# Turning nine of twelve quantized x tiles on VectorE inside the attention units instead of on TensorE after them

## The reference, cut to what matters

```python
xn = _layernorm(x, axis=-1)
s  = attention(xn)            # 32 query heads of 16, one shared key and value head, causal, then @ wo
h  = _linear8bit(xn, W1, b1)  # rows of xn quantized to 8 bits (absmax/127), columns above a threshold kept whole
y  = _linear8bit(h, W2, b2)
return x + s * silu(y)
```

## Time and profile before

| | us |
|---|---|
| median of 3 runs (lowest, highest) | 790.0 (789.12, 792.09) |
| the profiled execution, its own time | 790.14 |
| its span in the profile | 788.4 |
| busy: PE, DVE | 753.5 (96%), 650.9 (83%) |
| busy: ACT, POOL | 395.5 (50%), 273.5 (35%) |

### The profile page before, as it was taken

How to read it: one execution, slowest core, us unless ns; L and a number is a source line. 1 busy time by engine, 2 the same in 40 slices (tenths; PEclk the granted TensorE clock), 3 DMA queues, 4 the chain that set the end, 5 groups by cost and what they waited for, 6 DMA issues and landing times. The chain is left out here.

```text
span 788.4 us, 11979 instructions
## 1 busy us (share of the span) xinstructions
PE 753.5 (96%) x4133; PEld 568.3 (72%) x4133; DVE 650.9 (83%) x1115; ACT 395.5 (50%) x670; POOL 273.5 (35%) x349
## 2 busy tenths in 40 slices
PE   5999999999999999999899999999998999999995
PEld 4877665556767666766578878778886888888884
DVE  7988999999899999996448568597858998599957
ACT  4454066777776776677834435454563333132212
POOL 7213135555555555555432212222100000027404
PEclk9999699999999999999999999999998999999998
DMA  7431302332332233234465677646323778427972
GB/s 258 156 111 54 78 21 78 88 81 78 93 106 84 83 84 83 82 83 124 134 228 172 153 239 209 187 101 166 82 53 121 236 245 269 148 89 237 337 279 107
DMA packets 93772, 110.71 MB, mean 140 GB/s; under 512 B 43136, under 2 KB 50320, under 8 KB 92176
## 3 DMA queue, kind: packets, MB, share of 16 engines
q1 hardware_dynamic: 93712, 109.95, 45.8%
HBM read 56.43 MB, written 40.37 MB: 123 GB/s over the span
## 5 line engine op out<-in xcount | busy, mean ns | idle before, releaser
L933 DVE TENSOR_REDUCE rowmax<-ps 128x2 f32<-128x512 f32 (+3 forms) x384 | 210.3, 591 | 19.5 <-PE ps L1010 17.9
L854 ACT ACTIVATE probs<-ps 128x512 f32<-128x512 f32 (+1 forms) x352 | 174.9, 558 | 71.1 <-PE ps L1023 69.7
L1010 PE MATMUL ps<-km,stack 128*128 128x256 f32 (+3 forms) x512 | 149.7, 347 | 2.3 <-PEq L195 1.9
L1023 PE MATMUL ps<-stack,ks 128*128 128x512 f32 (+1 forms) x352 | 131.4, 383 | 2.8 <-ACT probs L854 2.7
L1010 PEld LDWEIGHTS ps<-km,stack 128*128 128x128 f32 (+1 forms) x512 | 94.2, 198 | 43.0 <-DVE rowmax L933 23.6
L836 POOL TENSOR_SCALAR_AFFINE_SELECT probs<-probs 128x512 f32<-128x512 f32 x128 | 81.0, 641 | 77.9 <-ACT probs L854 76.4
L1872 PE MATMUL ps<-big_h 128*128 128x512 f32 x256 | 99.9, 390 | 1.6 <-issue 1.2
L1874 PE MATMUL ps<-big_h,big_l 128*128 128x512 f32 x256 | 99.6, 389 | 0.0
L1873 PE MATMUL ps<-big_l,big_h 128*128 128x512 f32 x256 | 99.6, 389 | 0.0
L1036 PE MATMUL ps<-probs,vones 128*32 128x512 f32 (+3 forms) x1024 | 82.2, 439 | 0.2 <-POOL probs L836 0.2
L1023 PEld LDWEIGHTS ps<-stack,ks 128*128 128x128 f32 x352 | 66.5, 189 | 11.7 <-ACT probs L854 6.2
(11 more groups left out here) (227 smaller groups left out, 1375.3 us busy)
## 6 DMA issues: line engine op xcount, KB each, us to landing
stack<-big_h SPq DMA_DIRECT2D x128, 64.0 KB, 2.0
h_scratch<-hs SPq DMA_DIRECT2D x7, 1024.0 KB, 4.7
hload<-h_scratch SPq DMA_DIRECT2D x14, 512.0 KB, 5.3
xn_scratch<-xa SPq DMA_DIRECT2D x4, 1024.0 KB, 4.4
stack<-big_l SPq DMA_DIRECT2D x64, 64.0 KB, 2.0
xi<-xn_scratch SPq DMA_DIRECT2D x16, 256.0 KB, 2.7
xe_scratch<-xm SPq DMA_DIRECT2D x16, 256.0 KB, 2.3
w2n<-in_L_ffn_W_dram SPq DMA_DIRECT2D x4, 1024.0 KB, 6.6
```

The costliest lines, as they stand in the source:

```text
L854: nc.scalar.activation(probs[p][:, o:o + nh * w], ps[:, STB[n % NST], 0:nh * w], ACT.Exp).then_inc(s_exp, 1)
L933: nc.vector.tensor_reduce(dst, src, AX_X, ALU.max).then_inc(s_red, 1)
L1010: last = nc.tensor.matmul(dst, stack[u % 3][rows, hp, P * qt:P * (qt + 1)], km[rows, u // KT, p0:p0 + npar, keys], start=True, stop=True)
L1023: ins = nc.tensor.matmul(ps[:, STB[n % NST], 0:nh * w].rearrange("p (h q) -> p h q", h=nh), ks[:, u // KT, p, P * kt:P * (kt + 1)], stack[ ...
```

## The change

Tile i (0 to 8) is now turned at step 2 of unit 7 + i, and tiles 9, 10 and 11 at steps 386, 394 and 402. Turning is one DVE instruction, a transpose of 32 x 32 blocks from SBUF to SBUF, `tail_rows[:, 0]` to `tail_rows[:, 1]`. So that blocks alone are enough, the blocks already lie in their right places in DRAM: the store of `xm` becomes four DMAs, one for each 32 rows, which write runs of 32 elements (128 bytes). ACT makes the high part one step later (SBUF to SBUF), POOL the low part two steps later. SP issues the load of tile i six steps before, which is step 20 of the unit before. PE's four transposes a tile go.

```diff
+        HB, SQ = 4, 32
+        def x_stores(n):
+            return 16 * (HB * min(n, EARLY) + max(n - EARLY, 0))
-        def tail_tile(g, after=0):
-            i, r = divmod(g - after - CH * U - 1, TAIL_STEP)
-            return i if r == 0 and 0 <= i < EARLY else -1
+        TURN_AT, STEADY = 2, 9
+        def turned(g, after=0):
+            t = g - after
+            if t < CH * U:
+                i = t // CH - KT - 3
+                return i if t % CH == TURN_AT and 0 <= i < STEADY else -1
+            i, r = divmod(t - CH * U - TURN_AT, 8)
+            return STEADY + i if r == 0 and i < EARLY - STEADY else -1
 # SP
                         sp.wait_ge(s_xe, u + 1)
-                        sp.dma_start(xe_d[P * u:P * (u + 1), :], xm[:, :]).then_inc(s_xes, 16)
-                    i = tail_tile(g, -5)
+                        if u < EARLY:
+                            for b in range(HB):
+                                sp.dma_start(xe_d[P * u:P * (u + 1), :]
+                                             .rearrange("(a j) (k b i) -> b j k a i", a=HB, k=KT, b=HB)[b],
+                                             xm[SQ * b:SQ * (b + 1), :].rearrange("j (k a i) -> j k a i", k=KT, a=HB)
+                                             ).then_inc(s_xes, 16)
+                        else:
+                            sp.dma_start(xe_d[P * u:P * (u + 1), :], xm[:, :]).then_inc(s_xes, 16)
+                    i = turned(g, -6)
                     if i >= 0:
-                        sp.wait_ge(s_xes, 16 * (i + 1))
-                        if i >= 2:
-                            sp.wait_ge(s_tt, i - 1)
-                        sp.dma_start(tail_rows[:, i % 2, :], xe_d[P * i:P * (i + 1), :]).then_inc(s_tr[i % 2], 16)
+                        sp.wait_ge(s_xes, x_stores(i + 1))
+                        if i:
+                            sp.wait_ge(s_tt, i)
+                        sp.dma_start(tail_rows[:, 0, :], xe_d[P * i:P * (i + 1), :]).then_inc(s_tr, 16)
 # POOL
                         if u:
-                            pool.wait_ge(s_xes, 16 * u)
+                            pool.wait_ge(s_xes, x_stores(u))
+                    i = turned(g, 2)
+                    if i >= 0:
+                        pool.wait_ge(s_xh, i + 1)
+                        nc.gpsimd.tensor_tensor(big_l[:, :, P * i:P * (i + 1)],
+                                                tail_rows[:, 1, :].rearrange("p (k t) -> p k t", k=KT),
+                                                big_h[:, :, P * i:P * (i + 1)].bitcast(F32),
+                                                ALU.subtract).then_inc(s_xlo, 1)
 # ACT
-                    i = tail_tile(g, 1)
+                    i = turned(g, 1)
                     if i >= 0:
+                        act.wait_ge(s_mf, misc_at[("o", *divmod(i, QT))] + 1)
                         act.wait_ge(s_tt, i + 1)
                         nc.scalar.copy(big_h[:, :, P * i:P * (i + 1)],
-                                       ps[:, MAXB[i % NMAX], :].rearrange("p (k t) -> p k t", k=KT)).then_inc(s_xh, 1)
+                                       tail_rows[:, 1, :].rearrange("p (k t) -> p k t", k=KT)).then_inc(s_xh, 1)
 # DVE
-                    i = tail_tile(g, 2)
+                    i = turned(g)
                     if i >= 0:
-                        dve.wait_ge(s_xh, i + 1)
-                        nc.vector.tensor_tensor(big_l[...], ps[:, MAXB[i % NMAX], :]..., ALU.subtract)...
+                        dve.wait_ge(s_tr, 16 * (i + 1))
+                        if i:
+                            dve.wait_ge(s_xlo, i)
+                        nc.vector.transpose(tail_rows[:, 1, :], tail_rows[:, 0, :]).then_inc(s_tt, 1)
 # PE
                         if b == B - 1 and j == 1:
+                            pe.wait_ge(s_red, CH * U)
                             pe.wait_ge(s_xlo, EARLY)
-                    i = tail_tile(g)
-                    ... (wait for the load and the bank, four transposes into it)
```

More of the change, by code:

```diff
@@ L607, in block_layernorm_attention_ffn @@
         s_nm = sem("heads_divided")
-        s_tr = [sem(f"tail_rows_loaded{i}") for i in range(2)]
-        s_tt = sem("tail_rows_transposed")
+        s_tr = sem("x_blocks_loaded")
+        s_tt = sem("x_blocks_turned")
         s_w1n = [sem(f"w1_loaded{i}") for i in range(2)]
@@ L670, in block_layernorm_attention_ffn @@
         EARLY = NT - QT
-        TAIL_STEP = 2
+        def x_stores(n):
+            return 16 * (HB * min(n, EARLY) + max(n - EARLY, 0))
         W1_LOAD_AT, W1_SCALE_AT, W1_ROUND_AT = 21, 30, 31
@@ L762, in _ @@
                         sp.wait_ge(s_xe, u + 1)
-                        sp.dma_start(xe_d[P * u:P * (u + 1), :], xm[:, :]).then_inc(s_xes, 16)
-                    i = tail_tile(g, -5)
+                        if u < EARLY:
[7 more added lines that the diff above has]
+                    i = turned(g, -6)
                     if i >= 0:
-                        sp.wait_ge(s_xes, 16 * (i + 1))
-                        if i >= 2:
-                            sp.wait_ge(s_tt, i - 1)
-                        sp.dma_start(tail_rows[:, i % 2, :], xe_d[P * i:P * (i + 1), :]).then_inc(s_tr[i % 2], 16)
+                        sp.wait_ge(s_xes, x_stores(i + 1))
+                        if i:
+                            sp.wait_ge(s_tt, i)
+                        sp.dma_start(tail_rows[:, 0, :], xe_d[P * i:P * (i + 1), :]).then_inc(s_tr, 16)
                     if unit_at(g, XSTORE_AT + 1) == U - 1:
                         sp.wait_ge(s_xm, NT)
-                        sp.wait_ge(s_xes, 16 * (EARLY + 1))
+                        sp.wait_ge(s_xes, x_stores(EARLY + 1))
                         sp.dma_start(inlier_row[:, :], xe_d[P * EARLY:P * (EARLY + 1), :]).then_inc(s_xel[0], 16)
@@ L790, in _ @@
                                      ).then_inc(s_obt if n in TAIL_OUT else s_obs[n % 2], 16)
-                sp.wait_ge(s_xes, 16 * NT)
+                sp.wait_ge(s_xes, x_stores(NT))
             @block.gpsimd
@@ L1152, in block_layernorm_attention_ffn @@
         s_t2 = sem("absmax_transposed")
-        HB, SQ = 4, 32
         def w2_pieces(f):
```

## The result

The changed kernel takes 835.55 us (median of 4 runs, 833.78 to 838.57) against 789.56 us of the kernel before in the same comparison. The ratio is 1.058, 95% interval 1.055 to 1.060: 46 us slower. The forecast was 812. The way and the place of the wait were right, the forecast change was half of what came, and the time lies at the very end of the range.

A forecast was written before the change was run, and what follows sets the result against it. PE was taken to bound an attention unit at 18.30 us, with late loads stalling DVE and PE. Starting from 790.1 us, plus 28.2 lost in turned units, less 6.5 gained in the tail, gave 812 us (811.8), range 798 to 836.

The forecast's parts named there:

- PE bounds a unit, and follows DVE closely in its first steps: Mid-attention unit: PE busy for all 18.30 us, DVE 16.75; each early max piece needs DVE's reduction three pieces before.
- DVE wants the tile at 2.12 us into the unit, and SP is late because of the queries: Unit 14 as pattern: DVE wants the tile at 328.35; SP, after twelve queries, reaches the store only at 326.26.
- The load goes out 2.15 us into the unit: SP in turned units: four stores of 0.53 us each precede the load, which goes out at 328.38.
- It lands 2.8 us later: Load in turned units: takes 2.8 us to land (2.0 to 4.3), so DVE stands still for 2.8 us.
- Loss of a unit 3.3 us: Units turning tiles 0 to 7: PE's step 6 piece runs 3.2 us later, the next waits 0.1 more; 26.4 us over eight.
- That the clock falls: Rival for turned units: PE's idle lowers its clock, typically 2 us a unit, 16 over eight, giving 828 us; chance 0.25.
- Tile 8: 1.8 us: Last turned unit: its load follows a one-DMA store of 0.58 us, so 1.3 us of wait and a loss of 1.8.
- The new work costs 0.45 a unit if the load is on time: Other-side rival: only DVE's slot is lost in nine units, 4.1 us less 6.5, giving 787.7 us; chance 0.04.
- The four-part store costs nothing in units 2 to 6: Later landing delays POOL's mask: zero in units 2 to 6, hidden by the stall in units 7 to 13.
- The tail gives 6.5 us: Tail: 5.5 us of transposes plus 1.0 of waits go; bounds 4 to 9.6; three remaining tiles cost nothing.
- The short runs load the DMA engines: 128-byte-run stores: engines 0.99 busy at 151 GB/s against 0.73 at 249; at most a few tenths added to the landing.

The follow-up runs named there:

- experiment 12: turn22 with the tail tiles' low part on DVE, ACT's high part moved to step 10 and POOL's low part to step 12 of the next unit: 786.35 us.
- Experiment 1: Changed kernel with the loads of tiles 0 to 8 issued at step 9 of the unit before, ahead of the twelve queries: 795.46 us, ratio 1.0057.
- load_early: Kernel of Experiment 1: changed kernel with the loads of tiles 0 to 8 issued ahead of the queries and stores: 795.46 us, ratio 1.0057.
- experiment 2: Changed kernel with the store of xm again one plain DMA of 2 KB rows, the load left where it is: 807.59 us, ratio 1.021.
- experiment 4: Changed kernel with PE repeating the step 5 max-piece matmul 20 times in units 7 to 15 to fill its idle: 825.76 us.
- experiment 5: Changed kernel with both the load ahead of the queries and the plain one-DMA store of xm: 791.19 us, ratio 1.0015.
- turn22: later_xload with tile i turned at step 22 of unit 6 + i, ten tiles in units and two in the tail: 790.74 us, ratio 1.0014.
- experiment 3: Kernel before with only the store of xm in four parts for tiles 0 to 11: ratio 0.9999.
- experiment 8: load_early with tail tiles 9, 10 and 11 left out altogether: 793.17 us, ratio 1.0048.
- later_xload: Changed kernel with tiles loaded at step 1 and turned at step 10 of their unit, next xn load moved behind the queries: 790.14 us, ratio 1.0005.

## Why the prediction was half right

1. *PE bounds a unit, and follows DVE closely in its first steps.* Right. Units with nothing late return to 18.29 us (experiment 12).
2. *DVE wants the tile at 2.12 us into the unit, and SP is late because of the queries.* Right within 0.03 us: the wait begins at 299.88, 2.15 after the close at 297.73. Experiment 1 shows the queue position as the cause.
3. *The load goes out 2.15 us into the unit* (four stores of 0.53). Too small in the mean: it went out 1.8 to 3.2 us into units 7 to 14, 2.5 in the mean, 2.97 in unit 11. Four stores took 2.63 us in six of these units (0.66 each) and 3.75 in units 10 and 11. I took the price from stores with the same runs in another stage. Why they cost more here is open; so is why one store took about 1.7 us in units 10 and 11 (load_early has such units too). In units 7 to 11 SP reached the stores 0.6 to 0.9 us before the close, which made up for some of it; in units 12 to 14 it reached them at the close, as forecast.
4. *It lands 2.8 us later.* Too small by 0.5: 3.3 in unit 11, median 3.2 over all. Behind the plain store of experiment 2 it is about 3.1, so the 128-byte runs are not the reason. Terms 3 and 4 make the wait 3.7 us in the mean (4.15 in unit 11) instead of 2.8.
5. *Loss of a unit 3.3 us.* It was 5.9 in the mean of units 7 to 14. Idle of PE is 4.0 of it (3.2 forecast; 3.07 to 4.61) and the other 1.9 lie at the lower clock (0 forecast). Over all nine turned units the forecast loss was 28.2 us and the measured one 49.2: longer idle explains 5.8 of the gap, and the other 15.2 are what the lower clock covers. That the clock falls was written as a rival with a chance of 0.25 and a price of 2 us a unit; it fell in each of units 7 to 14, and experiment 4 gets back 1.5 a unit. The step that failed is this one: I priced the stall at a clock of 1.00, although the rows showed the lower clock after an idle of 1.9 us with thin work. The longer wait is not what brought it: units 7 and 8 had PE idle for 3.07 and 3.27 us, as forecast, and they have the lowest mean clock of all, 0.86. Unit 15, with an idle of 2.04 us, kept 1.00, and so did all units of experiment 2, with 0.99 to 2.37.
6. *Tile 8: 1.8 us.* 2.2.
7. *The new work costs 0.45 a unit if the load is on time.* 0.40 (experiment 5). I put it down to DVE's slot, and PE's wait of 0.2 us for DVE at the piece of step 6 bears that out for this place. What the prediction did not have is that the same price waits elsewhere: with DVE's turn in its idle (turn22) PE waits 0.22 us for ACT instead, and the 0.4 to 0.5 goes only when ACT's and POOL's parts move too. What ACT's copy and POOL's low part cost by themselves at steps 3 and 4 was not tried.
8. *The four-part store costs nothing in units 2 to 6.* Right (experiment 3; +0.3 us over five units).
9. *The tail gives 6.5 us.* It gave 3.0. With no tile in it the tail gives 5.4 (experiment 8), and PE's busy time falls from 40.5 to 35.3 us: about the 5.5 of the transposes, without the 1.0 for the waits. The other 2.4 us are the three tiles left behind, in part through the clock, whose mean in the changed kernel's tail was 0.96. I had them at nothing because each engine's share of busy time was low.
10. *The short runs load the DMA engines*. That stretch also holds issues of `w2n`, `h_scratch` and `w1n`, so it does not measure the stores alone. Units 3 to 5 do: the DMA share is 0.34 to 0.36 with the four-part store and 0.28 to 0.30 before, at the same 78 to 80 GB/s, by an estimate from these shares 1 us of all engines more for a tile. The direction is as I had it, and it had no price of its own.

The sum with the measured terms is 790 + 47.0 + 2.2 + 2.3 (units 1 to 6) - 3.0 - 0.4 = 838, the profiled execution's level (838.57, the highest of four; the median is 3 us lower, and 2.0 of the sum are unit 1, which is not the change's).

## What to carry to other kernels

A DMA's issue time is set by what stands ahead of it in its queue, not by the step at which the program writes it. Before moving work that waits for a load, read the issuing engine's own timeline and count the issues between the last wait and the load. Price a stall of several microseconds on TensorE with the return at half clock behind it. And when three engines take a small step each, look for the idle of each engine by itself; the step needs no common place.

## What the runs showed of the hardware

- The issue of a DMA of 64 KB in 128-byte runs took 0.63 us in the median of the changed kernel's 48 (0.62 to 1.75), the same in later_xload (0.62 to 1.30), and 0.53 for stores of a like form in the W1 stage.
- Idles of PE of 4.0 to 4.6 us (units 9 to 14) were followed by a mean clock of 0.93 in the unit, about 3 us of work at half speed; idles of 3.07 and 3.27 us (units 7 and 8) by 0.86, in unit 7 with the clock at 0.50 from 207 to 213. After 2.04 us (unit 15) it stayed at 1.00. In each of units 7 to 15, 20 repeated matmuls of 0.18 us kept it at 1.00 and gained 10 us over the run.
